# Half-row matmul pairs in three of four rounds of a fused Mamba, attention and expert kernel

## The chip, the cores and the metric

One NeuronCore of a Trainium2 chip (1 of 8) runs the whole kernel in one launch. The metric is the device time of that core in microseconds, the median of several executions. Profiles are of one execution each; their times are counted from the first instruction.

## The reference, cut to what matters

For eight sequences of 512 tokens and 256 features (x is 8x512x256), `xn = layernorm(x)`, and the output is

```
out = x + mamba(xn) + attention(xn) + experts(xn)
u = conv4(xn @ W_in + b_in) + conv_b          # 512 channels, taps at t, t-1, t-2, t-3
h_t = tanh(A) h_{t-1} + u_t * Bp;  y_t = Cp.h_t + Dp*u_t      # 16 states per channel
mamba = silu(y) @ W_out + b_out
attention = softmax(q k^T / 4) v              # 16 heads of 16, no output projection
experts = sum over the top 2 of 8 of gate_e * (xn @ W_e + b_e)
```

All in float32. The state recurrence is the same linear filter for all channels, so the kernel applies it as a Toeplitz product over time.

## The kernel before, in words

**Rounds.** `program` writes each engine's instructions out by hand, in 256 rounds (STEPS) and a tail. Round t has one pair of score products (`score`, L581 and L591): two heads, 48 rows each (three parts of a split that keeps float32 accuracy in fp32r products), one in rows 0 to 47 of the PE array, one in rows 64 to 111, into the two banks of SB. VectorE takes the row maxima of both (`largest`, L1049), and the next score pair waits for that, as SB is single. LAG = 11 rounds later the same product is made turned, with the maxima as two more rows (`turned`, L595 and L608), into the two banks of TB; ScalarE takes the exponent of both into Pt (L827), and the next turned pair waits for that. Each fourth round has the products of the exponents with the values (`values`, L612 and L624), for two rounds' heads and in four column strips of the array. Eight rounds are a group g: after them the maxima are transposed (unit X), split (mh, ml) and sent by four DMAs as rows into qst (`max_row`, L1260); the sums of a group are transposed (unit P) and divided (`normalise`, L950). For each group SP sends twelve DMAs that build the operand stacks (`half_stack`, L420), released by the last turned pair of the group three back.

**Units.** All other PE work is cut into units with one PSUM bank each, of three (FB): T (transposes of xn, 2 a batch item b), V (values and gate, 4), Q (queries and keys, 4), Z (the Toeplitz filter of xn, 2, twelve products), Y (W_in, 4), C (transposes of gate columns), M (experts, 16), O (W_out, 4), B and D at the start. Q, Y and M are six full-height products of 512 columns: two halves of the contraction, each as high x high, low x high, high x low (`three`, L460 to L464). M and O units are copied by ScalarE in two pieces (`mt_copy`, L667 to L674) and added by GpSimd (L1118). A Y unit is copied to uc, then VectorE makes four taps of the convolution (`conv`, L884) and one gating multiply (L1082), with a tanh on ScalarE between.

**What sets the order.** `plan` (L53) is a planner at build time. It knows a cost of each unit on PE and VectorE and a wished round (WANTED), and gives each round one to three units so that the work is spread evenly. Units are taken in the order of `32 * b + WANTED` when `soonest` allows. The last unit of a round is read by the other engines in the next round (`early`, L194), the others in the same (`late`, L199). A round of values gets no unit but B, X or P. On VectorE a round is: `largest`, taps, early units, gating, gate, layer norm, late units. The taps of a Y unit lie in the four rounds behind it. On ScalarE: early units, the exponent, the copy of sums, late units.

Of the kernel before, what the change touches and what calls it, by code (L numbers as in the profile page):

```python
# [15 lines left out]
LAG = 11  # L16
# [3 lines left out]
NM = 4  # L20
W_QK, W_VG, W_E0, W_E1, W_IN, W_OUT, W_E2, W_E3, W_Q0 = range(9)
W_E = (W_E0, W_E1, W_E2, W_E3)

Unit = namedtuple("Unit", "kind b i t read bank use frees item before")

COST = {"T": 0.45, "V": 0.75, "Q": 1.42, "Z": 2.05, "Y": 1.42, "C": 0.45, "M": 1.42, "O": 1.5, "B": 0.25, "D": 1.42,
        "X": 0.15, "P": 0.45}

VECTOR = {"T": {1: 0.7}, "V": {1: 0.2}, "Q": {1: 0.8}, "Z": {1: 1.4}, "P": {1: 0.7}, "X": {1: 0.3},
          "Y": {2: 1.1, 3: 1.1, 4: 1.1, 5: 1.1, 6: 0.85}}

WANTED = {("T", i): -30 for i in range(2)}
WANTED.update({("V", i): -30 for i in range(4)})
WANTED.update({("Z", i): -20 for i in range(2)})
WANTED.update({("Q", i): -30 for i in range(4)})
WANTED.update({("Y", i): 4 * i - 8 for i in range(4)})
WANTED.update({("M", i): 2 * i for i in range(16)})
WANTED.update({("O", i): i // 2 * 8 + 6 + i % 2 * 2 for i in range(4)})  # L40
# [3 lines left out]
         1: [("Q", 0), ("Q", 1)]}  # L44

# [6 lines left out]

def plan():  # L53

    steps = {t: [] for t in range(-2, END + 1)}
    at, xh, ln = {}, {0: -1}, {0: -1, 1: 6}
    for t, row in FIRST.items():
        steps[t] = [(k, 0, i) for k, i in row]
        at.update({u: t for u in steps[t]})
    todo = [(k, b, i) for b in range(NB) for k, i in WANTED if b == 0 or k != "B"]  # L60
    steps[STEPS + LAG - 1] = [("M", NB - 1, 15)]
    at["M", NB - 1, 15] = STEPS + LAG - 1
    todo = sorted((u for u in todo if u not in at), key=lambda u: 32 * u[1] + WANTED[u[0], u[2]])

    vector = [1.25 * (0 <= t < STEPS) for t in range(END + 40)]

    def load(kind, b, i, t):

        for k, us in VECTOR.get(kind, {}).items():
            vector[t + k] += us  # L70
        if (kind, i) == ("V", 3):
            for k in (3, 4, 5, 6):
                vector[t + k] += 0.6

    def after(key, k):
        return at[key] + k if key in at else END

    def soonest(kind, b, i):

        if kind == "T":  # L80
            return max([ln.get(b, END) + 5, 9] + [after(("M", b - 2, n), 1) for n in range(16) if b >= 2])
        if kind == "V":
            return max(after(("T", b, 1), 2), 32 * b - 18 if b > 1 else 0)
        if kind == "Q":
            return max(after(("T", b, 1), 1), 32 * b - 10 if i < 2 else 32 * b + 6 if b else 5 if i == 2 else 7)
        if kind == "B":
            return 6
        if kind == "Z":
            return max(xh[b] + 5, 4) if b in xh else END
        if kind == "Y":  # L90
            t = after(("Z", b, 1), 1) if i == 0 else after(("Y", b, i - 1), 4)
            return max(t, after(("B", 0, 3), 1)) if b == 0 else t
        if kind in "CM":
            return after(("V", b, 3), 8 if kind == "M" else 9)
        return max(after(("Y", b, i // 2 * 2 + 1), 9), after(("C", b, 0), 1))

    def fixed(t):

        pairs = (0 <= t < STEPS) + (LAG <= t < STEPS + LAG)
        return 0.43 * pairs + 0.8 * len(values_at(t))  # L100

    last, spent = STEPS + LAG - 4, 0.0
    for t in range(END):
        row = steps[t]
        left = sum(COST[u[0]] for u in todo) + sum(fixed(n) + (COST["X"] + COST["P"]) / 8 for n in range(t, last))
        share = left / max(last - t, 1)
        spent = min(spent, 1.0) + share + 0.7 * max(vector[t] - share, 0.0) - fixed(t) - sum(COST[u[0]] for u in row)
        for u in row:
            load(*u, t)
        g, rest = divmod(t - 8, 8)  # L110
        if rest == 0 and 0 <= g < NG:
            row.append(("X", g // 4, g))
            load(*row[-1], t)
            spent -= COST["X"]
        g, rest = divmod(t - LAG - 10, 8)
        if rest == 0 and 0 <= g < NG:
            row.append(("P", g // 4, g))
            load(*row[-1], t)
            spent -= COST["P"]
        bare = fixed(t) < 1.5 and not any(COST[u[0]] > 0.5 for u in row)  # L120
        while not values_at(t) and t != STEPS + LAG - 2:
            k = next((k for k, u in enumerate(todo) if soonest(*u) <= t and not (u[0] == "Z" and values_at(t + 1))), None)
            if k is None or spent < COST[todo[k][0]] / 2 - 1.2 * bare or len(row) > 2 and todo[k][0] != "B":
                break
            bare = False
            u = todo.pop(k)
            row.append(u)
            at[u] = t
            spent -= COST[u[0]]
            if u[0] == "Z":  # L130
                u = "Z", u[1], 1
                todo.remove(u)
                steps[t + 1].append(u)
                at[u] = t + 1
                break
            load(*u, t)
            if u[0] == "Y" and u[2] == 3:
                xh[u[1] + 1] = max(ln[u[1] + 1] + 5, t + 1)
                ln[u[1] + 2] = max(32 * u[1] + 64 - 29, xh[u[1] + 1] + 1)
                for k, us in ((0, 1.2), (1, 1.2), (3, 0.85), (4, 0.85)):  # L140
                    vector[ln[u[1] + 2] + k] += us
    assert not todo, todo
    for b in range(NB):
        assert max(at["Q", b, 0], at["Q", b, 1]) < 32 * b - 5 + 7 * (b == 0)
        assert max(at["Q", b, 2], at["Q", b, 3]) < 32 * b + 11
        assert b == 0 or at["C", b - 1, 0] < at["V", b, 3] + 6
        assert b < 2 or at["M", b - 2, 15] < at["V", b, 3] + 6
        assert b == 0 or xh[b - 1] + 4 < ln[b] + 5 and at["T", b - 1, 1] < ln[b] + 3

    units, n, item, uses, frees, held = {}, 0, 0, [0] * 3, [0] * 3, [None] * 3  # L150
    used, free = [-9] * 3, [-9] * 3
    for t, row in steps.items():
        units[t] = []
        for k, (kind, b, i) in enumerate(row):
            bank = min((j for j in range(3) if free[j] <= t), key=lambda j: used[j])
            n += 1
            used[bank] = n
            uses[bank] += 1
            frees[bank] += kind not in "MO"
            u = Unit(kind, b, i, t, t + (k == len(row) - 1), bank, uses[bank], frees[bank], item, held[bank])  # L160
            if kind == "Z":
                assert i == 1 or u.read == t + 1
                free[bank] = END if i == 0 else t
# [30 lines left out]
def early(t):  # L194

    return AT[t - 1][-1:] if t - 1 in AT else []
# [1176 lines left out]
```

## Time and profile before

| | |
|---|---|
| time, median of 3 runs | 787.6 us (786.55 to 788.08) |
| the profiled execution, span | 784.0 us, 3.6 below the median time |
| PE / VectorE / ScalarE / GpSimd busy | 96% / 74% / 68% / 50% of the span |
| granted TensorE clock, mean | 0.992 (full level, 2.4 GHz, from about 65 us on) |
| first round's score, last score | 18.9 us, 751.6 us |

The profile gives busy times by engine and by line, the waits of each engine with what released them, and a timeline. The start of a matmul's record says when the array was free for it; its duration has the fill and drain in it, so two records overlap, and the distance between starts is what a product costs. PEld are the weight loads. PE being busy 96% doesn't tell whether the products follow one another at their shortest distance.

### The profile page before, as it was taken

The numbers are of one execution on the slowest core, as the hardware profiler recorded it, in microseconds if no ns is written. First come the engines' busy times: TensorE is split into PE (matmuls) and PEld (weight loads), VectorE is DVE, ScalarE is ACT, GpSimd is POOL, SyncE is SP. The second block draws the span as 40 slices with busy tenths as digits, with TensorE's granted clock in tenths as the row PEclk, the third lists the DMA queues.
The fourth block names the chain that finished last, engine by engine and source line by source line (L and its number), as shares of the span: only waits on it lengthen the run. The fifth ranks groups of instructions, "written<-read, shape, count | busy, mean of one in ns | idle before, by whom it ended". The sixth has DMA issues, their size and how long they took to land.

```text
span 784.0 us, 13236 instructions
## 1 busy us (share of the span) xinstructions
PE 756.4 (96%) x4408; PEld 455.7 (58%) x4408; DVE 582.2 (74%) x846; ACT 534.5 (68%) x926; POOL 389.7 (50%) x522
## 2 busy tenths in 40 slices
PE   9889999999999999999999999989999999999996
PEld 7566656566555665556555565556655565555553
DVE  6679785977679765897759877698767987568920
ACT  5546775676666766777667776667666776767775
POOL 8347482456344834455346373445444473435654
PEclk9979999999999999999999999999999999999999
DMA  8302111122110221102111121103111111112000
GB/s 272 68 8 66 46 24 30 30 69 69 35 29 22 69 69 41 42 15 82 42 42 42 42 86 32 39 23 96 42 42 43 42 49 41 46 39 69 22 2 27
DMA packets 32465, 39.09 MB, mean 50 GB/s; under 512 B 8513, under 2 KB 18535, under 8 KB 32398
## 3 DMA queue, kind: packets, MB, share of 16 engines
q1 hardware_dynamic: 31418, 37.29, 18.1%
q10 hardware_dynamic: 980, 0.96, 0.6%
q8 instruction: 35, 0.57, 0.3%
q14 instruction: 32, 0.26, 0.1%
HBM read 8.74 MB, written 4.19 MB: 17 GB/s over the span
## 4 chain that ended last, share of the span: by engine, by line
PE 80%; DVE 13%; issue 3%; POOL 2%; ACT 2%; DMA 0%; ACTq 0%; DVEq 0%; POOLq 0%
PE PS L464 38%; PE PS L624 13%; PE SB L591 12%; PE TB L608 7%; PE PS L521 4%; DVE mx L1049 4%; DVE xn L1026 2%; DVE ys L900 2%; PE PS L480 2%; DVE qkl L926 1%; POOL acc L1118 1%; PE PS L631 1%; DVE xl L932 1%; PE PS L476 1%; PE PS L555 1%
## 5 line engine op out<-in xcount | busy, mean ns | idle before, releaser
L1049 DVE TENSOR_REDUCE mx<-SB 128x2 f32<-128x1024 f32 x256 | 312.6, 1221 | 145.2 <-PE SB L591 144.3
L1118 POOL TENSOR_TENSOR acc<-acc,mt 128x256 f32<-128x256 f32 x320 | 252.7, 798 | 244.4 <-ACT mt L674 181.7
L827 ACT ACTIVATE Pt<-TB 128x1024 f32<-128x1024 f32 x251 | 257.5, 1026 | 58.1 <-PE TB L608 54.5
L674 ACT ACTIVATE mt<-PS,cpad 128x256 f32<-128x256 f32 x256 | 107.4, 470 | 58.5 <-PE PS L464 56.5
L591 PE MATMUL SB<-kst,qst 48*128 48x512 f32 x512 | 128.2, 497 | 12.1 <-DVE mx L1049 11.7
L624 PE MATMUL PS<-Pt,V 128*17 128x512 f32 x1024 | 122.3, 595 | 0.0
L591 PEld LDWEIGHTS SB<-kst,qst 48*128 48x128 f32 x512 | 47.8, 183 | 122.4 <-DVE mx L1049 70.3
L464 PE MATMUL PS<-weh,xTh 128*128 128x512 f32 x256 | 109.8, 429 | 1.9 <-DVE xTl L913 1.2
L608 PE MATMUL TB<-qst,kst 50*128 50x512 f32 x502 | 101.3, 399 | 1.3 <-ACT Pt L827 1.3
L464 PE MATMUL PS<-wel,xTh 128*128 128x512 f32 x256 | 100.9, 394 | 0.0
L464 PE MATMUL PS<-weh,xTl 128*128 128x512 f32 x256 | 100.7, 393 | 0.0
L900 DVE SCALAR_TENSOR_TENSOR ys<-uc,cwc,ys 128x511 f32<-128x511 f32 (+2 forms) x96 | 87.4, 910 | 0.0
L464 PEld LDWEIGHTS PS<-weh,xTh 128*128 128x128 f32 x256 | 48.4, 189 | 29.5 <-issue 15.3
L624 PEld LDWEIGHTS PS<-Pt,V 128*17 128x17 f32 x1024 | 23.5, 96 | 63.0 <-issue 62.6
L1243 POOL TENSOR_TENSOR yl<-th,yh 128x512 fp32r<-128x512 f32 x32 | 42.9, 1339 | 31.6 <-ACT yh L760 31.6
L464 PEld LDWEIGHTS PS<-wel,xTh 128*128 128x128 f32 x256 | 48.1, 188 | 11.1
L464 PEld LDWEIGHTS PS<-weh,xTl 128*128 128x128 f32 x256 | 48.4, 189 | 7.0
L608 PEld LDWEIGHTS TB<-qst,kst 50*128 50x128 f32 x502 | 47.7, 186 | 5.9 <-ACT Pt L827 5.5
L1127 POOL TENSOR_TENSOR acc<-acc,at 128x256 f32<-128x256 f32 x31 | 23.1, 747 | 55.4 <-DVE at L960 54.6
L464 PE MATMUL PS<-wouth,yh 128*128 128x256 f32 x128 | 37.3, 292 | 0.3 <-DVE xl L932 0.3
L464 PE MATMUL PS<-woutl,yh 128*128 128x256 f32 x128 | 35.9, 280 | 0.0
L464 PE MATMUL PS<-wouth,yl 128*128 128x256 f32 x128 | 35.9, 280 | 0.0
(162 smaller groups left out, 1138.9 us busy)
## 6 DMA issues: line engine op xcount, KB each, us to landing
qst<-qkh SPq DMA_DIRECT2D x124, 64.0 KB, 2.3
kst<-qkh SPq DMA_DIRECT2D x124, 64.0 KB, 2.3
out<-acc SPq DMA_DIRECT2D x8, 512.0 KB, 2.8
qst<-qkl SPq DMA_DIRECT2D x62, 64.0 KB, 2.2
kst<-qkl SPq DMA_DIRECT2D x62, 64.0 KB, 2.3
acc<-in_x SPq DMA_DIRECT2D x7, 512.0 KB, 3.9
Bt<-in_wexp SPq DMA_DIRECT2D x2, 512.0 KB, 8.0
raw<-in_wexp SPq DMA_DIRECT2D x2, 512.0 KB, 8.5
```

The costliest lines, as they stand in the source:

```text
L464: ins = e.matmul(P, u, v, start=(start and k == 0), stop=(stop and k == n - 1))
L521: ins = e.matmul(P[:, lo:lo + n], p[:, c, fs], q[:, r:r + n], start=(k == 0), stop=(k == 11))
L591: ins = e.matmul(SB[:, h, :], qst[rows, g % 3, jj, 128 * a:128 * a + 128], kst[rows, g % 3, jj, :], start=True, stop=True)
L608: ins = e.matmul(turned_bank(t)[:, h, :], kst[rows, g % 3, jj, 128 * a:128 * a + 128], qst[rows, g % 3, jj, :], start=True, stop=True)
L624: ins = e.matmul(OB[32 * j:32 * j + 17, :], V[:, g // 4 % 2, a, 4 * (g % 4) + j, :], Pt[:, (2 * m + j % 2) % NP, j // 2, :], start=(a == 0 ...
L674: return e.activation(mt[:, item % NM, :], P, ACT.Copy, scale=scale)
L827: e.activation(Pt[:, T % NP, :, :], turned_bank(T)[:, :, :], ACT.Exp, scale=0.25).then_inc(s_ex, 1)
L900: ins = e.scalar_tensor_tensor(out=y[:, s:512], in0=v[:, 0:512 - s], scalar=cwc[:, d, 3 - s:4 - s], in1=y[:, s:512], op0=ALU.mult, op1=ALU ...
L1049: e.tensor_reduce(mx[:, g % 2, 0:2, 4 * jj + a], SB[:, :, :], AX.X, ALU.max).then_inc(s_mx, 1)
L1118: e.tensor_tensor(v, v, mt[:, item % NM, :], ALU.add).then_inc(s_mt, 1)
L1127: e.tensor_tensor(v, v, at[:, :].rearrange("p (a c) -> p a c", a=4), ALU.add).then_inc(s_ad, 1)
L1243: e.tensor_tensor(yl[:, d, :], th[:, :], F(yh[:, d, :]), ALU.subtract).then_inc(s_yl, 1)
```

## The change

The number of products and their results' sums stay; their form and order change.

- *Sides.* M, Q and Y units are made in half rows: contraction rows 0 to 63 in the lower half of the array and 64 to 127 in the upper, six products each. In the three rounds t+1, t+2, t+3 after a round t with t % 4 == 0 there are three units a, b, c: (a low, c up), (b low, a up), (c low, b up), each six pairs of half-height products (`side_by_side`). A unit's second half waits for its first.
- *The fourth round* (t % 4 == 0, LAG is now 12) has the values and all other units: P and X, or up to two of T, C and V, then at most one of Z, O, V, B (or an M where units are behind), at full height as before.
- T, C, V, X and P in these rounds use the two banks of TB (FB has five banks now): they wait for the round's exponent, and the next turned pair waits until they are read.
- *Taps* and gating are put by the planner where VectorE's planned time stays below 2.0 us, or 4.6 in a fourth round. A tap is 0.93 in the plan beside 1.25 for the maximum, so taps lie in fourth rounds. Only the first tap of a round stands ahead of the late units.
- zh and zl get memory of their own; a Z unit is read for itself; layer norm takes 8 rounds; X makes 16 rows instead of 72; score and turned products each increment their semaphore.

```diff
-LAG = 11
+LAG = 12
+CYCLE = 8
...
+    def most(t):
+        if t < 16:
+            return 2.6
+        return (4.6 if t % 4 == 0 else 2.0) - 1.0 * (t >= STEPS) * (t % 4 == 0)
...
+        elif t % 4 == 0:
+            room_tb = 2 if t % 8 == 4 or t > STEPS + LAG else 0
+            while room_tb:
+                u = take(lambda u: u[0] in "TCV" and soonest(*u) <= t and (u[0] != "T" or room_tb == 2 - u[2]))
...
+            left = sum(u[0] in "QYM" for u in todo)
+            slots = 3 * ((STEPS + LAG - t) // 4)
+            u = take(lambda u: u[0] in "ZOVB" and soonest(*u) <= t)
+            if u is None and left > slots:
+                u = take(lambda u: u[0] == "M" and soonest(*u) <= t)
...
+                    sides[t + 1], sides[t + 2], sides[t + 3] = (a, c), (b, a), (c, b)
...
+        FB = [P[:, :] for P in PS[1:4]] + [TB[:, h, :] for h in range(2)]
...
+            def side_by_side(low, up):
+                for u in (low, up):
+                    if u not in begun:
+                        bank_there(u)
+                        operands_there(u)
+                if low in begun:
+                    e.wait_ge(s_high, begun[low])
+                if up in begun:
+                    e.wait_ge(s_low, begun[up])
+                for k, ((o, v, w, _), (p, a, b, _)) in enumerate(zip(products(low), products(up))):
+                    below = e.matmul(o, v[0:64], w[0:64], start=(k == 0 and low not in begun), stop=(k == 5 and low in begun),
+                                     skip_group_check=True)
+                    above = e.matmul(p, a[64:128], b[64:128], start=(k == 0 and up not in begun),
+                                     stop=(k == 5 and up in begun), skip_group_check=True)
...
+            def bank_there(u):
...
+                if u.bank > 2 and u.t >= LAG:
+                    e.wait_ge(s_ex, u.t - LAG + 1)
...
+                for u in TURNED_AFTER.get(t, ()):
+                    e.wait_ge(*bank_read(u))
...
                 for m in values_at(t):
                     values(m)
+                if t in SIDES:
+                    side_by_side(*SIDES[t])
                 for u in AT[t]:
                     unit(u)
...
-                for s in (3, 2, 1, 0):
-                    for b, d in y_read(t - s - 1):
-                        conv(b, d, s)
                 for u in early(t):
                     if u.kind != "D":
                         unit(u)
...
+                taps = taps_at(t)
+                for b, d, k in taps[0:1]:
+                    conv(b, d, k)
                 for b, name in gate_at(t, "DVE"):
                     gate(b, name)
...
                 for u in late(t):
                     unit(u)
...
+                for b, d, k in taps[1:]:
+                    conv(b, d, k)
+                for b, d in gating_at(t):
```

## Rows read from the trace of the kernel before

**Rows 1.** The page: busy us, share of the span and instructions of each engine.

```profile
PE 756.4 (96%) x4408; PEld 455.7 (58%) x4408; DVE 582.2 (74%) x846; ACT 534.5 (68%) x926; POOL 389.7 (50%) x522
```

**Rows 2.** Windows, the steady stretch: us; busy (instructions) by engine; clock, DMA share, GB/s.

```profile
54.60:753.90 699.30, 685.48 (x4022) 407.61 (x4021) 542.07 (x761) 488.81 (x835) 346.04 (x457) 1.00 0.18 45
```

**Rows 3.** Waits of PE in 54.6 to 753.9 us: total, times, longest us.

```profile
PE SB L591 <- DVE mx L1049: 8.7, 14, 1.7
```

**Rows 4.** Timeline of PE: start us, us, engine line op out<-in shapes xcount.

```profile
300.59 0.40 PE L464 MATMUL PS<-wel,xTh 128*128 128x512 f32 x1
300.91 0.50 PE L591 MATMUL SB<-kst,qst 48*128 48x512 f32 x2
301.25 0.40 PE L608 MATMUL TB<-qst,kst 50*128 50x512 f32 x2
301.58 0.50 PE L464 MATMUL PS<-weh,xTh 128*128 128x512 f32 x1
301.92 0.39 PE L464 MATMUL PS<-weh,xTl 128*128 128x512 f32 x1
302.15 0.39 PE L464 MATMUL PS<-wel,xTh 128*128 128x512 f32 x1
...
303.16 0.49 PE L591 MATMUL SB<-kst,qst 48*128 48x512 f32 x2
...
305.66 0.50 PE L591 MATMUL SB<-kst,qst 48*128 48x512 f32 x2
```

**Rows 5.** Timeline of PE's weight loads in the same stretch.

```profile
300.91 0.19 PEld L591 LDWEIGHTS SB<-kst,qst 48*128 48x128 f32 x2 [0.37 <-issue]
301.02 0.19 PEld L608 LDWEIGHTS TB<-qst,kst 50*128 50x128 f32 x2
...
301.92 0.19 PEld L464 LDWEIGHTS PS<-wel,xTh 128*128 128x128 f32 x1
```

**Rows 6.** Timeline of VectorE: maxima and taps, 408 to 417 us.

```profile
408.18 1.23 DVE L1049 TENSOR_REDUCE mx<-SB 128x2 f32<-128x1024 f32 x1 [1.28 <-PE SB L591]
409.32 0.74 DVE L896 SCALAR_TENSOR_TENSOR ys<-uc,cwc,Bt 128x512 f32<-128x512 f32 x1
409.99 0.27 DVE L908 TENSOR_TENSOR ml<-PS,mh 16x128 fp32r<-16x128 f32 x1
...
415.25 1.21 DVE L900 SCALAR_TENSOR_TENSOR ys<-uc,cwc,ys 128x510 f32<-128x510 f32 x1
416.38 1.21 DVE L1049 TENSOR_REDUCE mx<-SB 128x2 f32<-128x1024 f32 x1
```

**Rows 7.** Timeline of ScalarE: the two copies of an M unit, then an exponent.

```profile
411.44 0.84 ACT L674 ACTIVATE mt<-PS,cpad 128x256 f32<-128x256 f32 x2 [0.56 <-PE PS L464]
412.16 1.02 ACT L827 ACTIVATE Pt<-TB 128x1024 f32<-128x1024 f32 x1
```

**Rows 8.** Timeline of PE: two scores, the second released by the maximum.

```profile
679.87 0.49 PE L591 MATMUL SB<-kst,qst 48*128 48x512 f32 x2
...
681.69 0.50 PE L591 MATMUL SB<-kst,qst 48*128 48x512 f32 x2 [0.53 <-DVE mx L1049]
```

**Rows 9.** Timeline of VectorE: the maximum of that second score.

```profile
682.23 1.23 DVE L1049 TENSOR_REDUCE mx<-SB 128x2 f32<-128x1024 f32 x1 [0.60 <-PE SB L591]
```

**Rows 10.** Timeline of PE: a P unit and what follows it.

```profile
400.91 0.66 PE L480 MATMUL PS<-ident,ot 128*128 128x128 f32 x4
401.32 0.48 PE L464 MATMUL PS<-weh,xTh 128*128 128x512 f32 x1
```

**Rows 11.** Timeline of VectorE: the division of that P unit.

```profile
401.92 0.25 DVE L956 RECIPROCAL rc<-PS 128x16 f32<-128x16 f32 x1
402.20 0.43 DVE L960 TENSOR_TENSOR at<-PS,rc 128x256 f32<-128x256 f32 x1
```

**Rows 12.** SP's timeline and page: a stack's first and last of twelve DMAs; issues (count, KB, us to landing).

```profile
393.64 1.28 SPq L437 DMA_DIRECT2D qst<-qkh  x2
...
401.06 0.60 SPq L437 DMA_DIRECT2D kst<-qkl  x1
qst<-qkh SPq DMA_DIRECT2D x124, 64.0 KB, 2.3
```

More of the change, by code:

```diff
@@ L50, in values_at, with normal_at @@
     return (2 * m, 2 * m + 1) if rest == 0 and 0 <= m < STEPS // 4 else ()
-def plan():
[L55 to L73, printed above, removed]
+def normal_at(t):
+    g, rest = divmod(t - LAG - 12, 8)
+    if t == STEPS + LAG + 2:
+        return NG - 1
+    return g if rest == 0 and 0 <= g < NG - 1 else None
@@ L93, in soonest @@
+            return max(t, after(("B", 0, 3), 1) if b == 0 else after(("O", b - 1, i // 2 * 2 + 1), 0))
         if kind in "CM":
[L94 to L109, printed above, removed]
+            late = {name: g[2 if b == 0 else 3] for name, g in ((g[0], g) for g in GATE)}
@@ new lines, in take @@
+    def take(test):
+        k = next((k for k, u in enumerate(todo) if test(u)), None)
+        return None if k is None else todo.pop(k)
+    for t, row in FIRST.items():
+        for k, (kind, i) in enumerate(row):
+            u = (kind, 0, i)
+            if u in todo:
+                todo.remove(u)
+            whole[t].append(u)
+            put(u, t, t + (k == len(row) - 1))
+    for t in range(2, END):
+        g = normal_at(t)
+        if g is not None:
+            u = ("P", g // 4, g)
+            whole[t].append(u)
+            put(u, t, t)
@@ L152, in plan @@
[L152 to L163, printed above, removed]
-                if i == 1:
-                    free[units[t - 1][-1].bank] = t
-            item += 2 * (kind in "MO")
-            held[bank] = u
-            units[t].append(u)
@@ new lines, in plan @@
+        assert b == 0 or done["C", b - 1, 0] < done["V", b, 3] + 9
+        assert b < 2 or done["M", b - 2, 15] < done["V", b, 3] + 9
+        assert b == 0 or xh[b - 1] + 4 < LN[b] + 5 and done["T", b - 1, 1] < LN[b] + 5
+    order = sorted(done, key=lambda u: (read[u], done[u] == read[u]))
+    ends = {t: [] for t in whole}
+    for u in order:
+        ends[read[u]].append(u)
+    item = {u: 2 * n for n, u in enumerate(u for u in order if u[0] in "MO")}
+    uses, frees, held, busy = [0] * 5, [0] * 5, [None] * 5, [-9] * 5
@@ new lines, in plan, with give @@
+    unit = {}
+    def give(key, banks, n):
+        kind, b, i = key
+        bank = min(banks, key=lambda j: busy[j])
+        busy[bank] = n
+        uses[bank] += 1
+        frees[bank] += kind not in "MO"
+        unit[key] = Unit(kind, b, i, at[key], done[key], read[key], bank, uses[bank], frees[bank], item.get(key), held[bank])
+        held[bank] = unit[key]
+    for t, row in whole.items():
+        for n, u in enumerate(row):
+            if CYCLE <= t < STEPS + LAG and done[u] == read[u]:
+                give(u, (4 if u[0] == "P" or u[0] != "X" and n else 3,), t)
+            else:
+                give(u, range(3), t + n / 8)
+        for u in sides.get(t, ()):
+            if u not in unit:
+                give(u, range(3), done[u] + 0.9)
@@ new lines, in plan @@
+    return ({t: [unit[u] for u in row] for t, row in whole.items()},
+            {t: [unit[u] for u in two] for t, two in sides.items()},
+            {t: [unit[u] for u in row] for t, row in ends.items()}, taps, gating, yhi, xh)
+AT, SIDES, READS, TAPS, GATING, YHI, XH = plan()
+UNIT = {(u.kind, u.b, u.i): u for row in READS.values() for u in row}
+TURNED_AFTER = {}
+for _u in UNIT.values():
+    if _u.bank > 2:
+        TURNED_AFTER.setdefault(max(_u.t + 1 - LAG, 0), []).append(_u)
+KRYLOV = {("T", 1): (1, 2), ("D", 0): (3,), ("D", 1): (4,), ("D", 2): (5,), ("D", 3): (6,)}
```

439 lines of the change are left out of this document (265 added, 174 removed), and 7 rows, old and new, of the table GATE.

## The prediction

> **What bounds the kernel now.** I read the page first: TensorE (PE) is busy for 96% of the span, VectorE 74%, ScalarE 68% [rows 1]. Then the windows: the steady stretch, from round 8 to the last score, is 699.3 of 784.0 us, with PE busy 98% of it at the full clock [rows 2]. It holds 248 rounds, which is 2.82 us a round or 11.28 us for a group of four. The largest wait of PE there, for the row maxima, is 8.7 us [rows 3]. So PE's own time is the bound, and the question is what PE's time consists of. A busy PE is not a PE at its peak, so I go by the distance between starts. In [rows 4] a full-height product follows another after 0.23 us, which is 512 columns at 2.4 GHz and a little. But the last full product to the score pair takes 0.32, score to turned pair 0.34, turned pair to the first full product 0.33, and from there to the second 0.34. The round from 300.91 to 303.16 has eight slots (two pairs, six products): 8 x 0.232 = 1.86, and it takes 2.25. **The two changes between half-height and full-height work cost 0.39 us a round.** [Rows 5] show why: the loads of the score pair start with the score itself, 0.32 after the last full product, so they weren't hidden; the loads of the turned pair start 0.11 later, and 0.23 after those the turned pair starts (301.02, 301.25). Both matmuls of a pair are recorded as one start, so a pair costs what one full product costs.
>
> **The change, part by part.**
> The sum is made against the profiled execution (span 784.0); the median of the runs, 787.6, is 3.6 above it, which I take as fixed.
>
> *Half rows in three of four rounds.* M, Q and Y (24 units a batch item, 192 in all, 190 outside the start) leave their own full-height rounds. Three of them fill three rounds as 18 pairs, the same streaming as 18 full products, and as score, turned and these six pairs are all half-height, no change is left in those rounds. From round 8 there are some 64 groups, so 192 such rounds: 192 x 0.39 = 75 us less. How long a pair takes in a chain of pairs the trace shows only for one step, 0.23 after its loads [rows 5]; the bounds are 0.23 and the 0.34 from score to turned [rows 4]. I take 0.23, as the missing 0.11 is seen to be the uncovered load of the pair before.
>
> *The fourth round.* It keeps one entry and one exit, and gets one more change, from the values (four column strips) to the full-height units behind them; before, those rounds held little but values. I price it with the 0.10 that first products lose in [rows 4]: 64 x 0.10 = 6 us more. Bounds 0 and 0.2 (13 us).
>
> *T, C, V, X and P in TB's banks.* These units now wait for the exponent of their own round. At the end of a group two units (b and c) end together, and ScalarE copies both before it starts that exponent. The copies of an M unit begin 0.72 before the exponent behind them [rows 7], so the exponent begins at about 0.2 + 2 x 0.72 = 1.6 us after the score's start, and its 1.02 [rows 7] end at 2.7. PE comes to these units after two pairs and the values: score to score is 2.50 in a round of values alone [rows 4], of which 0.1 is the exit, so 2.4. PE then stands for some 0.25 us in seven of eight fourth rounds (all with P or X, three of four of the others): 0.22 x 62 groups = 12 us (steady groups 62). Bounds: 0 (copies of Q and Y are shorter) and 0.6 (27 to 35 us) if the copies don't overlap. Before the next turned pair, VectorE must have read these banks; what covers that is the full-height unit behind them.
>
> *Taps in the fourth rounds.* The dependence to follow is score, maximum, score. The maximum starts 0.54 after the score (681.69, 682.23), and where PE waits for it, scores are 1.82 apart (679.87, 681.69) [rows 8, 9]: that loop is just under the 1.86 of a light round, so light rounds have no slack to catch up in. VectorE's instructions overlap a little: 1.14 from a maximum to the next instruction, 0.67 for a tap that stands alone [rows 6]. But a tap took 1.13 (415.25 to 416.38), and I take 0.84 as a mean between those. A light round then has room for 0.7 us of other vector work (1.86 less 1.14), which Q's low half (0.67 by the spacing of such rows) just fits. The fourth round with P: maximum until 0.54 + 1.14, a tap to 2.5, then it waits for P's transposes (2.7 + 0.41 [rows 10] + 0.25 for the end of them), divides (0.7 [rows 11]) and takes X to 4.3, then the second tap to 5.1. With a Z or O unit behind them (8.25 and 6 full widths, 1.9 and 1.4 us) PE is at its next score at 4.7 to 5.3, whose maximum is due 0.54 later: covered. Without such a unit, PE is ready at 3.2 and VectorE at 5.1: 1.2 to 1.3 us lost. There are 48 Z and O for 64 fourth rounds, so two of eight lack one: 2 x 1.2 x 62 / 8 = 19 us. Bounds: 0, if whole M units fill these rounds, which the planner does when units are behind, and 45 us with all taps at 1.13.
>
> *Light rounds' leftovers.* Normalisation, gate and Q's low halves now and then pass 0.7 us; 0.08 us a group, 5 us. Bounds 0 and 25.
>
> *The stacks.* A stack's twelve DMAs take SP from 393.64 to 401.66, and 2.3 us more to land [rows 12], so 10.3 us. They are released by the last turned pair of three groups back, in round 8g-5, and are needed by the score of round 8g: four light rounds and a fourth one, less 0.7: 4 x 1.86 + 4.9 - 0.7 = 11.6 us. Covered by 1.3 us, at cost 0; if that fourth round is a short one (2.6), 1.0 us is late, at most 32 times, 32 us. The four rows of maxima behind them on SP have three light rounds and the rest of a fourth, 5.6 + 2 us; they follow on the same queue, and nothing else is queued there but stores and loads that are needed a batch item later. I take 0.
>
> *Separate zh, zl; Z in one go each; a score increment per matmul; the smaller transpose for X.* No matmul more or less; 0, hidden behind PE, whose stream has no wait there.
>
> *Gone:* of the 8.7 us of waits for maxima [rows 3], 6 us, as in light rounds PE no longer waits there. *One more round of lag* at the end: a turned pair and its exponent, 1 us.
>
> Sum: -75 + 6 + 12 + 19 + 5 + 0 - 6 + 1 = -38, so 784.0 - 38 = 746 of span, **750 us** of time. A group comes to 10.6 us.
>
> **Rivals.**
> *PE alone decides.* Nothing in the fourth round waits: -75 + 6 - 6 + 1 = -74, and 8 us of waits as now [rows 3]: -66, or 722. For it: the longest list of PE's waits is that short now, and the chain to the next maximum has been covered. Against: a PE that does its work in 10 us a group leaves VectorE and ScalarE less cover. Chance 0.17.
>
> *VectorE's queue sets the rounds (slower).* The place is the step from one maximum to the next. Where an instruction beside GpSimd's work takes 1.13 rather than 0.67 [rows 6], a light round is 1.14 + 1.13 = 2.27 us, no shorter than the round of before (2.25). With one of three light rounds so (0.41 us) and 0.5 us in the fourth round for its taps, a group costs 0.91 x 62 = 56 more, less the 5 counted: 801 us. It decides from 0.6 us a group, which eats the forecast's gain. For it: a tap took 1.13 in these rows, the taps are now bunched, and GpSimd's work is denser in time. Against: taps are kept out of light rounds. Chance 0.15. The Trainium skill, "TensorEngine Tiling (Array Packing)", section PSUM Bottleneck, says that packing speeds up TensorE but not the emptying of PSUM; the trace agrees in that the maximum alone takes 1.23 [rows 6] of what would be a 1.86 us round. By that rule the time would be this rival's.
>
> *Pairs don't chain at 0.23 (slower too).* If each pair's loads stay uncovered, each of the 18 pairs takes 0.34: a light round is 8 x 0.34 = 2.72 against 2.25, so 192 x 0.47 = 90 us more, and with the 6, 12, 19, -6 and 1 of above: 910 us. The half-height work doesn't do what it says then. Against: [rows 5] show the turned pair's loads under the running score. Chance 0.06. The Trainium skill, "TensorE: Matmul & The Clock Gate", section The mechanism, says that a weight load overlaps a running matmul only where the row groups differ. Here the trace disagrees: full-height loads start with the full-height matmul in front of them (both at 301.92 [rows 4, 5]), in the same rows. By that rule the time would be this rival's.
>
> *The exchange evens out*, the losses of the fourth round being at their upper bounds together: within 0.2% (about what a measurement of this kernel can tell from no change), 0.05. The forecast itself: 0.57.
>
> **How the numbers follow.** Faster: 0.17 + 0.57 = 0.74. Same 0.05. Slower: 0.15 + 0.06 = 0.21. The range goes down to 722, the first rival. Upwards, the exponent, the taps, the light rounds and the stacks can be 23, 26, 20 and 32 us above their terms; two fifths of all four together is 40, which gives 790; the rest, the two slower rivals but for a little, is left out: **722 to 790**.
>
> **What would show it.** Right: light rounds with score starts 1.86 to 1.95 apart and pairs 0.23 to 0.24 apart; no change of height in them; a fourth round of about 4.9 us; PE waits of some 30 to 40 us in all, on the exponent at lines of X, P, T, V and on the maxima behind the fourth round; VectorE over 75% busy. Wrong: pairs 0.34 apart (third rival); light rounds at 2.1 or more with PE waiting for the maxima (second); PE waits below 15 us (first); a score that waits for a DMA of the stacks.

## The result, and the profile after

| | before | after |
|---|---|---|
| time, median (range) | 787.8 us (786.6 to 789.4) | 798.4 us (797.9 to 801.4) |
| ratio, 95% interval | | **1.0147** (1.0119 to 1.0174) |
| profiled execution: time, span | span 784.0 | 801.4, span 799.6 |
| score of round 8, of round 16 | 54.7, 79.7 us | 58.0, 81.3 us |
| round 8's score to the last score | 696.9 us | 698.1 us |
| last score to the end | 32.4 us | 43.4 us |

The change makes the kernel slower by 10 to 12 us; the forecast was 38 us faster. The profiled execution of after is the longest of its four, so of its terms some 3 us are its own. "Round" below is from one score's start to the next; "fourth round" is one with t % 4 == 0, and "light rounds" are the three behind it (first, second, third).

The page's busy row, to be laid beside [rows 1]:

```profile
PE 731.9 (92%) x5562; PEld 492.5 (62%) x5562; DVE 576.1 (72%) x845; ACT 535.0 (67%) x926; POOL 410.6 (51%) x522
```

Windows, with the columns of [rows 2]: the steady stretch (score of round 8 to the last score), and four shorter ones.

```profile
58.00:756.20 698.20, 655.27 (x5105) 438.80 (x5107) 517.97 (x743) 483.57 (x824) 355.79 (x449) 0.98 0.18 45
20.00:60.00 40.00, 28.54 (x130) 19.35 (x128) 28.34 (x47) 17.04 (x34) 14.82 (x17) 0.85 0.18 36
60.00:100.00 40.00, 35.30 (x243) 25.02 (x244) 28.79 (x40) 24.40 (x43) 14.51 (x17) 0.85 0.21 54
587.00:602.00 15.00, 6.76 (x34) 5.40 (x36) 7.39 (x17) 2.57 (x3) 1.19 (x6) 0.54 0.23 77
760.00:799.60 39.60, 28.18 (x186) 18.23 (x178) 15.84 (x23) 21.20 (x36) 19.84 (x21) 0.87 0.08 28
```

PE's waits in the steady stretch, beside [rows 3]:

```profile
PE SB L765 <- DVE mx L1222: 22.2, 14, 12.5
PE TB L711 <- issue: 5.9, 21, 0.4
PE TB L783 <- DVE xTl L1090: 3.7, 3, 1.2
PE TB L718 <- issue: 3.3, 5, 2.1
```

From the score of round 8 to the last score the kernel takes 698.1 us, 1.2 more than before (the window of [rows 2] runs to 753.9, 2.3 us past the last score, so its 699.3 is not to be laid beside the 698.2 here). The whole gain is gone inside it, and the start and the tail add 14 more. The named waits are far less than the 48 us that are missing, so they don't tell it alone. What does is the distance between starts. Two light rounds and the fourth behind them, for [rows 4]:

```profile
399.67 0.40 PE L765 MATMUL SB<-kst,qst 48*128 48x512 f32 x2
399.91 0.41 PE L783 MATMUL TB<-qst,kst 50*128 50x512 f32 x2
400.15 0.49 PE L677 MATMUL PS<-weh,xTh 64*128 64x512 f32 x1
400.16 0.50 PE L679 MATMUL PS<-weh,xTh 64*128 64x512 f32 x1
400.49 0.39 PE L677 MATMUL PS<-weh,xTl 64*128 64x512 f32 x1
400.50 0.39 PE L679 MATMUL PS<-weh,xTl 64*128 64x512 f32 x1
400.72 0.39 PE L677 MATMUL PS<-wel,xTh 64*128 64x512 f32 x1
...
401.64 0.41 PE L765 MATMUL SB<-kst,qst 48*128 48x512 f32 x2
...
403.51 0.41 PE L765 MATMUL SB<-kst,qst 48*128 48x512 f32 x2
403.74 0.45 PE L783 MATMUL TB<-qst,kst 50*128 50x512 f32 x2
404.12 1.91 PE L798 MATMUL PS<-Pt,V 128*17 128x512 f32 x16
405.96 0.50 PE L663 MATMUL PS<-Rh,xh 128*128 128x512 f32 x1
...
408.09 0.50 PE L765 MATMUL SB<-kst,qst 48*128 48x512 f32 x2
```

The half rows do what was forecast: a pair follows a pair after 0.23, score to turned is 0.24 where it was 0.34, and light rounds take 1.97 (here with one uncovered step, 0.34 from 400.15 to 400.49) and 1.87. From 403.51 a fourth round takes 4.58, without P or X. Over rounds 16 to 255 the mean light rounds are 2.27, 1.97 and 1.91, and the fourth 5.14; without the one stall below it is 4.97, where 4.9 was forecast. So the fourth rounds came out nearly as said, and the light ones, forecast at 1.86, did not. A group of four from round 8 to 196 takes 11.11 us (before 11.59), not 10.6, and at round 196 the kernel is 19 us ahead. It then loses all of it: from round 196 to 200 it takes 23.4 us (before 12.4), and from there to round 255 152.5 (before 140.0).

**A fourth round with P and X**, all engines:

```profile
716.25 0.40 PE L765 MATMUL SB<-kst,qst 48*128 48x512 f32 x2
...
716.49 1.57 ACT L851 ACTIVATE mt<-PS,cpad 128x256 f32<-128x256 f32 x4
...
716.86 1.91 PE L798 MATMUL PS<-Pt,V 128*17 128x512 f32 x16
...
717.93 1.04 ACT L1004 ACTIVATE Pt<-TB 128x1024 f32<-128x1024 f32 x1
...
719.07 0.63 PE L711 MATMUL TB<-ident,ot 128*128 128x128 f32 x4 [0.30 <-issue]
...
719.74 0.26 DVE L1129 RECIPROCAL rc<-TB 128x16 f32<-128x16 f32 x1 [1.13 <-PE TB L711]
...
721.80 0.50 PE L765 MATMUL SB<-kst,qst 48*128 48x512 f32 x2
```

The exponent starts 1.68 after the score and ends 2.72 after it; PE's transposes follow 0.1 later. The forecast had 1.6, 2.7 and a wait of 0.25; the row has 0.30 of idle time. This step is right nearly to the row. What it costs by the distance between starts is more, as the runs with the exponent first show below.

**The load of x for the last batch item**, SP and VectorE:

```profile
579.10 1.29 SPq L557 DMA_DIRECT2D qst<-qkh  x2
...
586.18 0.59 SPq L557 DMA_DIRECT2D kst<-qkl  x1
586.87 0.53 SPq L1445 DMA_DIRECT2D out<-acc  x1
589.83 0.39 SPq L1425 DMA_DIRECT2D acc<-in_x  x1
...
593.43 0.43 DVE L1186 BATCH_NORM_STATS2 st<-acc 128x6 f32<-128x256 f32 x1 [13.02 <-DMA acc<-in_x]
...
595.24 0.80 PE L765 MATMUL SB<-kst,qst 48*128 48x512 f32 x2 [12.46 <-DVE mx L1222]
```

Batch item 7 is loaded into the accumulators of item 4, once these are stored. With taps only in fourth rounds, item 4's last Y and O units are late and its store is due in round 195 (before 174), which is the round in which item 7's layer norm begins. The store stands behind a stack's DMAs, the load waits for the store, VectorE for the load, the maximum is queued behind VectorE's wait, and PE stands for 12.5 us. The clock then falls to half: 0.54 over 587 to 602, pairs 0.42 apart.

### The profile page after: what moved, and what is told of

Read it like the earlier page. It is cut to its first block, busy times and chain, and to the rows that moved or that the text cites. A ratio compares the mean times of both kernels' runs of the same rounds, so it can differ in the third digit from the quotient of the medians.

```text
span 799.6 us, 15797 instructions
## 1 busy us (share of the span) xinstructions
PE 731.9 (92%) x5562; PEld 492.5 (62%) x5562; DVE 576.1 (72%) x845; ACT 535.0 (67%) x926; POOL 410.6 (51%) x522
## 4 chain that ended last, share of the span: by engine, by line
PE 77%; DVE 10%; issue 5%; ACT 3%; DMA 1%; SPq 1%; POOL 1%; ACTq 0%; POOLq 0%; DVEq 0%
PE PS L677 20%; PE PS L798 12%; PE PS L663 10%; PE PS L679 10%; PE SB L765 9%; PE TB L783 7%; DVE mx L1222 4%; PE TB L711 2%; PE TB L663 2%; DVE ys L1077 2%; PE TB L706 1%; PE PS L805 1%; DVE xTl L1090 1%; SPq L557 1%; ACT Pt L1004 1%
## 5 line engine op out<-in xcount | busy, mean ns | idle before, releaser
L1289 POOL TENSOR_TENSOR acc<-acc,mt 128x256 f32<-128x256 f32 x320 | 262.1, 829 | 207.5 <-ACT mt L851 163.7
L765 PE MATMUL SB<-kst,qst 48*128 48x512 f32 x512 | 115.2, 441 | 29.2 <-DVE mx L1222 28.7
L851 ACT ACTIVATE mt<-PS,cpad 128x256 f32<-128x256 f32 x256 | 102.9, 474 | 20.4 <-PE PS L679 18.6
L679 PE MATMUL PS<-weh,xTh 64*128 64x512 f32 x256 | 103.2, 403 | 0.0
L677 PE MATMUL PS<-weh,xTh 64*128 64x512 f32 x256 | 102.8, 402 | 0.0
L679 PE MATMUL PS<-wel,xTh 64*128 64x512 f32 x256 | 102.0, 398 | 0.0
L679 PE MATMUL PS<-weh,xTl 64*128 64x512 f32 x256 | 101.5, 397 | 0.0
L677 PE MATMUL PS<-weh,xTl 64*128 64x512 f32 x256 | 100.9, 394 | 0.0
L677 PE MATMUL PS<-wel,xTh 64*128 64x512 f32 x256 | 100.8, 394 | 0.0
L1077 DVE SCALAR_TENSOR_TENSOR ys<-uc,cwc,ys 128x511 f32<-128x511 f32 (+2 forms) x96 | 83.0, 864 | 0.9
L798 PEld LDWEIGHTS PS<-Pt,V 128*17 128x17 f32 x1024 | 23.4, 96 | 61.7 <-issue 59.6
L783 PEld LDWEIGHTS TB<-qst,kst 50*128 50x128 f32 x500 | 49.7, 190 | 12.4 <-issue 8.6
L677 PEld LDWEIGHTS PS<-weh,xTh 64*128 64x128 f32 x256 | 47.9, 187 | 14.5 <-DVE zl L1107 3.0
L677 PEld LDWEIGHTS PS<-wel,xTh 64*128 64x128 f32 x256 | 47.8, 187 | 6.5
L677 PEld LDWEIGHTS PS<-weh,xTl 64*128 64x128 f32 x256 | 48.4, 189 | 4.6
L679 PEld LDWEIGHTS PS<-wel,xTh 64*128 64x128 f32 x256 | 48.2, 188 | 3.6
```

Source lines behind the costliest of these rows:

```text
L677: below = e.matmul(o, v[0:64], w[0:64], start=(k == 0 and low not in begun), stop=(k == 5 and low in begun), skip_group_check=True)
L679: above = e.matmul(p, a[64:128], b[64:128], start=(k == 0 and up not in begun), stop=(k == 5 and up in begun), skip_group_check=True)
L765: e.matmul(SB[:, h, :], qst[rows, g % 3, jj, 128 * a:128 * a + 128], kst[rows, g % 3, jj, :], start=True, stop=True).then_inc(s_S, 1)
L783: e.matmul(turned_bank(t)[:, h, :], kst[rows, g % 3, jj, 128 * a:128 * a + 128], qst[rows, g % 3, jj, :], start=True, stop=True).then_inc( ...
L798: ins = e.matmul(OB[32 * j:32 * j + 17, :], V[:, g // 4 % 2, a, 4 * (g % 4) + j, :], Pt[:, (2 * m + j % 2) % NP, j // 2, :], start=(a == 0 ...
L851: return e.activation(mt[:, item % NM, :], P, ACT.Copy, scale=scale)
```

## The experiments

All kernels compute the whole output. Ratios are to the kernel of before on the same chip, where 1.0147 is the change as it is. Theory after the result: half rows bring about what was forecast, but late taps (store, load, tail) and longer fourth rounds eat it. Rivals: the half rows are worth much less; or the exponent wait is the loss.

### The stall alone (e_ln7)

```diff
 LN = {b: max(32 * b - 29, 0) for b in range(1, NB)}
+LN[7] = 199
```

> Layer norm of the last batch item starts four rounds later (LN[7] = 199), all else as in the changed kernel. Theory (late store): the one wait of VectorE of 13.0 us for the last x (PE then 12.5 us behind it, and 13.7 us at half clock after it) goes, as x is there by round 199; about 14 us less than the changed kernel, some 784 us. The plan of the end shifts by a few rounds, which may give back 3. Rival (the wait only covered others): the time stays within 4 us of 798.

Measured: 793.5 us, 1.0071 (1.0046 to 1.0097). The 12.5 us wait is gone, but the time fell by 5 to 6 us only. Layer norm and all behind it came later: rounds 200 to 255 take 155.4 us (152.5 in after), six M units are planned behind round 255 where after has one, and the last score to the end is 43.8 us. A stall removed by lateness returns in part as lateness.

### Half rows undone, twice (e_full, f_full)

The same plan and the same rounds, each unit at full height in one go, one in each of the three light rounds; e_full on e_ln7, f_full on e_taps22 (below).

```diff
             def side_by_side(low, up):
...
-                for k, ((o, v, w, _), (p, a, b, _)) in enumerate(zip(products(low), products(up))):
...
+                u = waiting.pop(0)
+                in_one(u).then_inc(s_full[u.bank], 1)
```

> As e_ln7, with the three units of a group made one in each of the three rounds at full height (six products of 128 rows), everything else the same. Theory (a change of height costs 0.39 us a round): 192 x 0.38 = 73 us more than e_ln7, some 857 us, light rounds at 2.25. Rival (VectorE's chain sets the light rounds anyway): under 30 us more.

> As e_taps22 (taps allowed in light rounds), with the units of the sides one a round at full height. Theory (what half rows are worth is the changes of height, as far as no other engine sets a round): in a plan without a late VectorE they are worth more than the 45 us of e_full against e_ln7; some 60 us, so 844 us. Rival (the fourth rounds' waits take the same part in any plan): 45 us again, 829.

Measured: e_full 838.9 us, 1.0644 (1.0620 to 1.0668); f_full 829.8 us, 1.0556 (1.0527 to 1.0585). Against their partners, half rows are worth 45 and 48 us: the largest term of the sum was 27 to 30 us too large. In f_full's timeline the rounds of before are back, 2.27 and 2.27 with the old 0.33 at each change:

```profile
401.23 0.50 PE L753 MATMUL SB<-kst,qst 48*128 48x512 f32 x2
401.57 0.40 PE L771 MATMUL TB<-qst,kst 50*128 50x512 f32 x2
401.90 0.50 PE L663 MATMUL PS<-weh,xTh 128*128 128x512 f32 x1
402.24 0.39 PE L663 MATMUL PS<-weh,xTl 128*128 128x512 f32 x1
402.47 0.40 PE L663 MATMUL PS<-wel,xTh 128*128 128x512 f32 x1
...
403.50 0.51 PE L753 MATMUL SB<-kst,qst 48*128 48x512 f32 x2
...
405.77 0.50 PE L753 MATMUL SB<-kst,qst 48*128 48x512 f32 x2
```

The second result: **the new plan without half rows is 44 us slower than before** (1.0556). Rounds 16 to 255 take 715.3 us in f_full and 671.9 in before. Some 16 of these 43.4 are products that now lie in these rounds and lay in the start or the tail (an estimate, their numbers times their shortest distances, 0.232 us for 512 columns). The rest, some 27, is lost between products: 8 at score to turned (0.37 on the mean where it was 0.34) and 7 from the values to the exponent-bound units (0.67 where 0.53 is reached when the exponent is ready, 51 times). The other 12 were not separated.

### The exponent ahead of the copies (e_exp, f_exp)

In the fourth rounds (FIRSTEXP: t % 4 == 0 between rounds 17 and 255) ScalarE makes the exponent before it reads the early units; e_exp on e_ln7, f_exp on e_taps22.

```diff
+                if FIRSTEXP(t):
+                    exponent()
+                    read_early()
+                else:
+                    read_early()
+                    exponent()
```

> As e_ln7, with ScalarE's exponent ahead of the copies of units b and c in fourth rounds. Theory (units in TB's banks wait for that exponent): the first of them starts 0.43 after the last values instead of 0.83, and 0.4 x 55 rounds = 22 us go, some 762 us. Rival (the next turned pair, or VectorE's reading of these banks and the taps behind it, is the next to end last): less than 6 us go.

> As e_taps22, with the exponent ahead of the copies in fourth rounds. Theory (in e_exp the wait only moved: the first light round grew by what the fourth lost, as the copies then stand ahead of the next exponent): again within 3 us of e_taps22. Rival (in e_exp it was VectorE, crowded in the fourth rounds, that took the gain): with taps in light rounds 10 us or more go.

Measured: e_exp 793.7 us, 1.0069 (1.0050 to 1.0088), no gain over e_ln7; f_exp 779.3 us, 0.9916 (0.9888 to 0.9944), where its partner e_taps22 (below) has 0.9946; the intervals overlap. The fourth rounds fell (4.97 to 4.78, 5.09 to 4.80) and the first light rounds rose (2.30 to 2.51, 2.27 to 2.37), the copies that free two banks now being behind the exponent. In f_exp the fourth rounds of 16 to 255 give 17.4 us in all and the light rounds take 11 of them back. The wait is real, and larger than the idle time in its row: from the last value product to the first transposes it is 0.90 us on the mean in e_taps22 (0.84 in after) and 0.53 in f_exp, 51 times, so 19 us (16 in after). But most of it is exchanged, not saved.

### Taps in light rounds too (e_taps22), and fewer in fourth rounds (f_cap)

```diff
-        return (4.6 if t % 4 == 0 else 2.0) - 1.0 * (t >= STEPS) * (t % 4 == 0)
+        return (4.6 if t % 4 == 0 else 2.2) - 1.0 * (t >= STEPS) * (t % 4 == 0)
```

(f_cap: 3.8 in place of 4.6 as well. A planned 2.2 lets one tap stand beside the maximum: 1.25 and 0.93.)

> The changed kernel with the planner's cap on VectorE in light rounds raised from 2.0 to 2.2 us, so that a tap fits beside the maximum there. In this plan the O units of the last item end in round 256 instead of 271, and the fifth item is stored in round 177 instead of 195. Theory (taps confined to fourth rounds are what runs late): no wait for x, the end from the last score 8 to 11 us shorter, and light rounds with a tap 0.1 to 0.2 longer (some 100 of them, 10 to 20 us): 780 us, and below the kernel before. Rival (VectorE's chain is dear in light rounds): light rounds with taps at 2.3, nothing gained, 795 or more.

> As e_taps22, with the planner's cap on VectorE in fourth rounds lowered from 4.6 to 3.8 us, which moves taps from there into light rounds. Theory (taps behind the late units end after PE is ready for the next maximum, so they cost in fourth rounds, and little in light ones): 3 to 8 us less than e_taps22. Rival (a light round with a tap loses as much as it relieves): no less, or up to 5 more.

Measured: e_taps22 784.1 us, **0.9946** (0.9922 to 0.9970); f_cap 779.9 us, 0.9924 (0.9894 to 0.9953). One number of the planner turns 1.5% slower into 0.5% faster. The tail falls from 43.4 to 33.9 us, item 4's store is due in round 177 rather than 195, and the stall is gone. The gain lies at the end, where lateness would put it: against after, rounds 16 to 196 take 9.7 us more, as more of the work is done there, rounds 196 to 255 take 14.8 less and the tail 9.5 less. The light rounds don't suffer on the mean: 2.27, 1.95 and 1.88, as before the edit. Taken singly, those with a tap are a little longer: in f_cap, which has 66 such, the second light round is 2.07 with a tap and 1.89 without, the third 1.89 with and without. First light rounds of 3.6 to 4.7 us come once a batch item, with a tap in them; but they stand behind T units with no large unit to cover VectorE's reading of TB, and after has two like them (rounds 45 and 77, 4.2 and 4.4) with no tap. So a tap in a light round costs 0 to 0.2 us, and the rival that put VectorE's queue into the light rounds had the wrong place. Kept out of there, taps are late.

### The start (f_start, g_idle)

f_start leaves the second Z unit out of round 4; g_idle adds, on f_cap, idle products in PE's waits of rounds 3 to 12.

```diff
+                u = take(lambda u: soonest(*u) <= t and not (u[0] == "Z" and mine))
```
```diff
+                idle_turns({4: 14, 12: 9}.get(t, 0))
...
+                idle_turns({3: 8, 5: 7, 6: 6}.get(t, 0))
```

> As e_taps22, with the second Z unit of the first batch item in round 5 instead of 4, as in the kernel before. Theory (round 4 takes 10.0 us instead of 4.6 as PE waits for the filter's low half and then makes both units, part of it at half clock): round 5 takes over most of it; round 8 begins 1 to 3 us earlier, and a stretch at half clock may go; 782 us. Rival: nothing measurable.

> As f_cap, with products that are thrown away (128 columns of the unit matrix, into the bank of the values, which is not yet in use) in the waits of PE in rounds 3 to 6 and 12, as many as fill them. Theory (three stretches at half clock between 36 and 79 us follow PE's waits there, and work made in them costs double): the stretches at half clock fall from 42 us by 20 or more, and 5 to 10 us go against f_cap. Rival (round starts there are set by VectorE, so a slow PE costs nothing): within 2 us of f_cap.

Measured: f_start 782.1 us, 0.9943 (0.9919 to 0.9968), not told from e_taps22, though round 16 starts 3.6 us earlier. g_idle 774.3 us, 0.9832 (0.9810 to 0.9853), 6 to 7 us below f_cap. The two windows of g_idle, whose clock is 0.81 and 0.85 in f_cap:

```profile
20.00:60.00 40.00, 35.33 (x206) 26.54 (x207) 29.94 (x51) 17.59 (x35) 14.16 (x16) 0.93 0.17 32
60.00:100.00 40.00, 37.54 (x299) 26.37 (x296) 33.61 (x45) 28.40 (x48) 17.00 (x19) 0.98 0.23 56
```

Stretches at the half level within the span fell from 40.2 us in f_cap to 22.7 (before had 13.2, the early ones ending at 54.1 us and not at 65; after had 55.1). Round 16 starts at 76.5 us, 4.8 earlier than in f_cap. The start does cost, through its waits and the clock behind them.

### Exponent-bound units behind the large one (g_order)

```diff
-                for u in AT[t]:
+                for u in sorted(AT[t], key=lambda u: CYCLE < t < STEPS and t % 4 == 0 and u.bank > 2):
```

> As f_cap, with T, C, V, X and P behind the large unit of a fourth round instead of ahead of it. Theory (the wait for the exponent is one of order: the large unit can cover it, but then nothing covers the reading of TB's banks): the wait ahead of the first transposes goes (0.4 us in 45 rounds), and the next turned pair waits 0.7 to 1.2 us for VectorE, so 15 to 35 us more than f_cap. Rival (the next turned pair is late anyway): 10 us less.

Measured: 784.0 us, 0.9948 (0.9930 to 0.9965), 2 us slower than f_cap if anything. Its waits of PE from 58 to 740 us, with new first rows:

```profile
PE TB L783 <- DVE ml L1085: 10.0, 30, 0.3
PE TB L783 <- DVE xTl L1090: 8.3, 7, 1.2
PE TB L783 <- DVE G L1098: 4.5, 14, 0.3
```

The fourth rounds fall from 5.08 to 4.79 and the first light round rises from 2.16 to 2.57. The forecast had said that the full-height unit behind these units covers VectorE's reading of TB. That is so: without this cover the next turned pair waits, and it costs what the exponent's wait had. It does not cost the 15 to 35 us more that were expected.

### The parts together (g_best, g_all)

g_best has the exponent first, the caps 3.8 and 2.2, and one Z unit in round 4; g_all adds idle products.

> The three small gains together: taps in light rounds with a cap of 3.8 us on fourth rounds, the exponent first in fourth rounds, the second Z unit in round 5. Theory (they lie in different places, but exponent and taps share the first light round): 2 to 6 us less than f_cap, 775 us. Rival (as with e_exp, the gain moves into the first light round): no less than f_cap.

> g_best with the thrown-away products of g_idle in PE's waits of rounds 3 to 6 and 12 (fewer in 5 and 6, where less is waited). Theory (half clock and the fourth rounds' waits are separate losses): 4 to 7 us less than g_best, some 762 us, with one or two of its three early stretches at half clock gone. Rival (with the Z units apart, VectorE sets the early rounds): within 2 us of g_best.

Measured: g_best **767.4 us, 0.9743** (0.9723 to 0.9763); g_all 766.7 us, 0.9746 (0.9724 to 0.9768). This version beats both kernels. Its page and its waits in the steady stretch:

```profile
PE 725.7 (95%) x5568; PEld 491.2 (64%) x5568; DVE 569.3 (75%) x845; ACT 530.8 (69%) x926; POOL 381.8 (50%) x522
...
PE TB L788 <- DVE xTl L1105: 9.3, 6, 1.7
PE TB L723 <- issue: 2.1, 1, 2.1
PE TB L788 <- DVE ml L1100: 2.1, 7, 0.3
```

The fourth round is 4.80 and the light rounds 2.24, 2.00 and 1.90. The light rounds still pay for the exponent's place, but less: 2.24 against 2.16 in f_cap for the first of them, 2.00 against 1.97 for the second (f_exp against e_taps22: 2.37 and 2.27, 2.01 and 1.95). That fewer taps stand in the round ahead is a likely reason, and not shown. By the spans of the profiled executions (e_taps22 783.8) f_exp brought 6.5, f_cap 6.0 and f_start 3.8 us, and all three together 20.0; by the ratios 2.4, 1.7, 0.2 and together 16. Singly each was near what a comparison can tell; together they are not. The idle products add nothing here; what they gave the start (2.0 us by round 16) the tail lost (35.0 us against 32.3, 15.9 of them at the half level against 6.5).

### What the start and the tail hid (h_tail, h_start, h_both)

All on the kernel of before.

```diff
-    last, spent = STEPS + LAG - 4, 0.0
+    last, spent = STEPS - 5, 0.0
```
```diff
-            return after(("V", b, 3), 8 if kind == "M" else 9)
+            return max(after(("V", b, 3), 8 if kind == "M" else 9), 16 if kind == "M" and i > 3 else 0)
```

(The first with the line that sets the last M unit to the end taken out.)

> The kernel of before, whose planner ends its work with round 251, so that no M or O unit is left for the rounds after 255 (before had seven M and one O there, in rounds that hold only a turned pair and values). Same products, same full height. Theory (the start and the tail of before hid products at no cost; taking them out costs their streaming): seven M units are 7 x 6 x 0.23 = 9.7 us, of which the shorter tail gives a part back: 5 to 9 us slower, 793 to 797. Rival (a unit costs the same wherever it stands, so it is only moved): within 2 us of before, 786 to 790.

> The kernel of before with four M units ahead of round 16 instead of eight. Theory: these four stood in gaps in which PE waits for the first copies, maxima and stacks, so taking them to steady rounds costs up to 4 x 1.4 = 5.6 us: 2 to 6 us slower, 790 to 794. It may be less, where the gaps lie at half clock and the start gets shorter by what the four took. Rival: within 1.5 us of before.

> Both at once: no M or O after round 255 and four M ahead of round 16, which is about how the changed kernel spreads its work, with full-height units and the order of before. Theory: 8 to 15 us slower than before, 796 to 803, which is that share of the 44 us by which the changed plan with full-height units was slower. Rival: within 2 us of before; then the whole 44 us come from the order inside the steady rounds.

Measured: h_tail 805.4 us, 1.0233 (1.0211 to 1.0255); h_start 785.6 us, 0.9987 (0.9977 to 0.9997); h_both 804.9 us, 1.0241 (1.0221 to 1.0261). The theory holds for the tail and falls for the start. Four M units moved out of the start cost nothing: rounds 16 to 255 take 671.0 us with them, 671.9 without. (All three plans also move two V units into the start, an estimated 1.4 us of products, so it is emptied by about 4 us rather than 5.6.) Eight units moved out of the tail cost 19 us, about twice what I gave them; the tail without them is only 1.7 us shorter (30.7 against 32.4). Rounds 16 to the last score take 14.6 us longer, and 7.0 are lost ahead of round 16, where the moved order makes PE wait 2.94 us for a gate and go on at the half level:

```profile
60.00:100.00 40.00, 36.34 (x183) 22.19 (x182) 32.21 (x49) 25.59 (x46) 21.22 (x27) 0.91 0.19 48
```

h_both starts round 16 only 1.0 us later, and there rounds 16 to the last score take 20.3 us longer for twelve units more and two V units less (12 x 6 x 0.232 = 16.7 us of streaming, less 1.4). The cleanest comparison is h_both with h_start, which differ in the eight units of the tail alone: 19.3 us, as from before to h_tail (19.1). So units that are taken out of the tail cost their full streaming (8 x 6 x 0.232 = 11.1 us) and more, 19 us for eight; what the other 8 us are, a new order or more waits, stays open. f_full's plan has five units less in the tail (two M and one O in place of seven and one): 7 us by streaming, 12 at that rate, of its 44 us.

## Why the prediction was wrong

By its own steps, ratios taken as shares of 788 us:

| step | forecast | measured | by |
|---|---|---|---|
| half rows in light rounds | -75 | -48 (-45) | f_full, e_full |
| rest of the plan: height +6, exponent +12, taps +19, light rounds +5, waits -6, round +1 | +37 | +44 | f_full against before |
| stacks, stores and loads, lateness | 0 | +16 | after against e_taps22 |
| sum | -38 | +12 (by medians +10.5) | |

**The largest miss is "192 x 0.39 = 75".** The price of one round was right where the light round is free to take it: 2.25 became 1.87. But over rounds 16 to 255 there are 180 light rounds, which makes 70 (5 us). The first of three follows full-height work and keeps an uncovered step, 1.97 rather than 1.86: what I booked to the fourth round once lies in both (7 us, leaving 63). The light rounds' measured gain is 53.2 us, by the round times of f_full and e_taps22. The missing 10 us I put down to rounds that something else sets, copies or VectorE's reading; that is argued and not separated. And the fourth rounds grew by 7.7 us with the half rows. The way for that is the exponent: units b and c now end together, and both are copied ahead of it, so that the values reach the transposes after 0.90 us rather than 0.67, which is 12 us in 51 rounds. 53.2 less 7.7 is the 45.5 that rounds 16 to 255 gained.

**The second is a zero: "nothing else is queued there but stores and loads that are needed a batch item later. I take 0."** I placed the taps in the fourth rounds and priced only what they cost there, never what their lateness does: twenty taps and gating steps a batch item for its eight fourth rounds fill what the planner allows, so each item's last Y and O units slip, its store meets the next load, and the tail grows by 11 us. e_taps22 shows 16 us for it, by changing one number. The rounds around the stall confirm the way: 12.5 us of wait, half the clock after it. e_ln7, which took only the stall, got 5 to 6 us.

**The third, +37 for the plan, came out at +44, partly by luck.** The exponent's wait was sized rightly to the row (0.25 forecast, 0.30 measured); its total is 7 us in f_full, 16 in after and 19 in e_taps22, around the 12. (By my own numbers 0.22 x 62 is 13.6, not 12; the half rows were counted in 64 groups and the rest in 62; and the mean of a tap's 0.67 and 1.13 is 0.90, not 0.84. None of this changes the miss.) The taps' 19 us weren't found as such; in their place 7 to 12 us come from products that left the tail, which I didn't price at all. Some 9 us of products that left the start are in the 44 too, and h_start says that such a move can be free; what these cost stays open.

**The rivals.** Pairs that don't chain: refuted, 0.23 at every covered step of the rows above; 0.23 is also what f_full's full-height products take, loads included (402.24 to 402.47). The Trainium skill, "TensorE: Matmul & The Clock Gate", section The mechanism, says in one line that loads overlap only where row groups differ; these rows disagree with that line. (The same section names a background weight buffer as a second way, which would agree; the prediction left that out.) PE alone (722): the waits were not short. VectorE's queue (801) came nearest in time and even in its cause, the taps, but not in its mechanism: with taps allowed there the light rounds kept their means of 2.27, 1.95 and 1.88, and the time went by lateness and the tail. What was named as a sign of being right was mostly there (pairs, a fourth round of 4.97, waits of some 40 us in all). Light rounds of 1.86 to 1.95 were there in the median of the second and third only (1.89 and 1.87, the first 1.97), and VectorE was busy 72%, not over 75%. A sign for the tail and for the store was not among them, and that is where the sign of the result was decided.

**Left open**: the price of the products that left the start, and 12 us lost between products in f_full; together some 20 of the plan's 44 us.

## What to carry to other kernels

A price per round holds only for the rounds that are free to take it: count those and see in which of two neighbouring rounds each change of form is paid. When work is confined to fewer slots, follow the last piece of it through to what it releases (a store, a load into the same memory, the tail), since an engine that is 72% busy on average can be full in exactly the slots allowed. And where PE has slack at the start or the end, check whether a new plan still uses it: eight units taken out of the tail cost 19 us.

## What the runs showed of the hardware

- Two half-height matmuls in disjoint rows chain with other pairs at 0.23 us, as full-height products do, and with the same 0.39 record. Where the step is not covered, mostly at a change of height, either takes 0.33 to 0.34.
- At the half level (1.2 GHz) pairs are 0.42 apart and records 0.62 long. Before two of the stretches in after, PE had waited: 3.19 us ahead of 39.87, and 12.46 us ahead of 595.24. From there products went at the half level until 44.8 and 601.3. A wait of 2.94 us in h_tail, whose clock over 60 to 100 us was 0.91, is also followed by such records (0.63 long, behind a first of 0.80).
- ScalarE's instructions overlap a little: the four copies of 128x256 above took 1.57 us together, and the exponent behind them starts 1.44 after the first, 0.13 before their end.
